# A selective scan: weighings on GpSimd, five polynomial steps on VectorE, front products first on TensorE, two pairs of input banks

## The chip, the core and the metric

The kernel runs on one core of a Trainium2 chip. The metric is the device time of one execution in microseconds. Times of runs are medians; one further execution was taken with the hardware profiler, and all rows below come from that one.

## The reference

Two transformer-like layers over x of shape (8, 512, 128). Layer 0 is a differential attention and a feed-forward network; layer 1 is a selective scan and a mixture of 64 experts. The change lies in the scan (and in one step at the end of the feed-forward network, which prepares the first batch of the scan):

```python
u = silu(conv3(h, conv_w))                     # h: layer-normed x, modulated; 3 taps over time
Bcoeff, Ccoeff = split(u @ W_bc + b_bc)        # 16 + 16 rows over time
A = -exp(A_log)
dt = softplus((u @ W_dt + b_dt) @ W_dtp + b_dtp)
# for each of the N = 16 states n, along time t:
#   h_n[t] = exp(A[:, n] * dt[t]) * h_n[t-1] + Bcoeff[n, t] * dt[t] * u_or_h[t]
y = sum_n Ccoeff[n, t] * h_n[t]  +  h * Dcoeff
x = x + gate * y
```

## The kernel before

The program is a sequence of phases: attention, feed-forward network, scan, experts. Inside a phase each engine has its own list of instructions and the engines meet by semaphores only; the order on an engine is the order in which the code is written. The feature axis (128) lies on the partitions and the 512 time steps along the free axis.

**Rounds and pairs.** The function `scan` runs one round for each of the 8 batches, r = 0 to 7, and a short last one. In a round the 16 states are taken in 8 pairs, m = 0 to 7, so that a tile of a pair is 128x1024. Flags tell what else a round does: `ahead` (r up to 5) prepares batch r + 2, `back` (r up to 6) finishes the step length of batch r + 1, `post` (r from 1) finishes the output of batch r - 1.

**What happens with a pair.** SyncE loads the rows of B and C, spread over all partitions, into `brow` and `crow`, 512 KB each, two places each (L1538); in rounds 0 to 3 its queue also carries the experts' weights, behind pairs 2 and 5. ScalarE makes `dA` = exp(A dt), two places (L1701). VectorE makes `dBx` = dtxb * brow in PSUM, in a single place (`enter`, L1739), and runs the scan over `dA` and `dBx` (`run`, L1749). The states of even pairs go to `gate_a0`, those of odd pairs to two places of `hs`. Even pairs are weighed with C by VectorE: `ch` = gate_a0 * cb (L1756), where `cb` is a copy of `crow` in PSUM, made by ScalarE (L1705). Odd pairs are weighed by GpSimd, straight from `hs` and `crow` (L1592). TensorE adds the `ch` tiles up in PSUM with an identity matrix (`add_pair`, L1630), two pairs behind.

**What else is in a round.** The step length is a softplus: ScalarE makes `zb` and `ee` = exp(-|z|); a polynomial in `ee` of 10 coefficients gives log(1 + ee). GpSimd begins it: one first step (L1198), then six pairs of a product and an addition (L1203, L1204) and a last product (L1208), spread between its four weighings; each instruction waits for the one before it through a semaphore. VectorE does the last two steps after pair 6 (L1186, `pl` = (pl + c) * ee), then `dt` = max(zb, 0) + pl (L1187) and `dtxb` = dt * hT in PSUM (L1189). VectorE normalizes batch r + 2 after pair 0 (`front.norm`, L1019, four instructions on 128x128) and adds the residual after pair 7 (L1729, one input in PSUM). In round 0 it also makes the statistics of batches 4 to 7. TensorE turns, convolves and projects the batch ahead (`turn`, `conv`, `bc_rows`, `z`) in between the sums; `silu` on ScalarE loads an activation table before and after. In rounds 1 to 6 ScalarE and GpSimd also split the experts' weights into two f16 parts (GpSimd: L1585, after weighing 7).

The end of the feed-forward phase does the same polynomial for batch 0 on GpSimd and VectorE, beside the last gating (`w_experts` <- sine, L1432, four instructions; the tiles of the expert weights are lent to that phase, hence the name) and `relu` (L1363).

## Time and profile before

| | us |
|---|---|
| median of 3 runs | 1761.32 (1758.82 to 1764.29) |
| profiled execution | 1767.51 |
| its span, first to last instruction | 1765.5 |
| mean granted clock of TensorE | 0.875 |
| busy in the span: TensorE, VectorE, ScalarE, GpSimd | 1325.0, 1247.3, 1064.9, 891.0 |
| scan phase in it, first to last scan | 995.0 to 1322.6 |

No engine is busy all the time, and each phase has another bound; for the change only the rows of the scan and of the end of the phase before it count. In rows in order of time the first number is the start, the second the time that the row covers; "x2" behind it are two instructions merged in one row. A number in square brackets is how long the engine was idle before, and for whom. Two rows of one engine can overlap by about 0.1 us.

### The profile page before, as it was taken

Reading aid. Unit: us, or ns where it says so; the run is one execution under the profiler, and the core shown is the slowest. Engines: PE = TensorE matmul, PEld = TensorE weight load, DVE = VectorE, ACT = ScalarE, POOL = GpSimd, SP = SyncE. Lnnn points to the kernel's source line nnn. Section 1 sums busy time; section 2 is a strip of 40 time slices with the busy share of each in tenths; the row PEclk is TensorE's granted clock in tenths of the full one; section 3 lists DMA queues with packets and bytes.
Section 4 is the critical chain, followed back from the end, with each engine's and each line's share of the span. In section 5 each row is a group of like instructions: output and inputs, shape, how many; then the busy total and the mean of one; then the engine's idle time right before and its main releaser. Section 6 shows DMA issues by size and latency. Waiting matters only on the chain. (4 is left out here: it accounts for less than half of the span.)

```text
span 1765.5 us, 29658 instructions
## 1 busy us (share of the span) xinstructions
PE 1325.0 (75%) x8526; PEld 587.4 (33%) x8589; DVE 1247.3 (71%) x2064; ACT 1064.9 (60%) x1633; POOL 891.0 (50%) x849
## 2 busy tenths in 40 slices
PE   4587888888888888764665466766555898988898
PEld 3233333333333333332333222222222344444443
DVE  4667767676767667853787688888994666665654
ACT  2277666666667676653554445555533677776686
POOL 3033525252525252433886355565632666766677
PEclk8599999999999899986787777787887999999999
DMA  4231313131313132100000476665654666765675
GB/s 130 72 114 46 106 34 106 37 108 38 108 40 99 42 89 63 39 2 0 1 0 1 133 225 217 221 221 201 210 202 98 164 171 163 184 168 153 173 191 131
DMA packets 123690, 198.73 MB, mean 113 GB/s; under 512 B 24604, under 2 KB 60088, under 8 KB 123576
## 3 DMA queue, kind: packets, MB, share of 16 engines
q1 hardware_dynamic: 122136, 195.08, 38.3%
q10 hardware_dynamic: 1440, 2.10, 0.4%
q8 instruction: 76, 1.25, 0.3%
q14 instruction: 38, 0.31, 0.1%
HBM read 167.76 MB, written 28.84 MB: 111 GB/s over the span
## 5 line engine op out<-in xcount | busy, mean ns | idle before, releaser
L959 DVE TENSOR_REDUCE bmax<-p1b 128x4 f32<-128x512 f32 x640 | 410.8, 685 | 140.1 <-PE p1b L704 135.4
L642 ACT ACTIVATE pT<-p2b 128x512 f32<-128x512 f32 x640 | 349.1, 602 | 193.4 <-PE p2b L756 192.2
L1918 POOL TENSOR_TENSOR hid_l<-e_hid,hid_h 128x1024 f16<-128x1024 f32 (+1 forms) x136 | 281.1, 2075 | 132.0 <-ACT hid_h L2060 131.4
L2176 DVE TENSOR_TENSOR e_hid<-ub,share 128x1024 f32<-128x1024 f32 x128 | 156.1, 1223 | 150.4 <-ACT ub L2073 129.4
L593 POOL CAST nsp<-qneg 128x16 bf16<-128x16 f32 x64 | 12.6, 197 | 442.9 <-DVE qneg L970 442.9
L1630 PE MATMUL yb<-ch,ident 128*128 128x512 f32 x256 | 156.3, 750 | 66.4 <-POOL ch L1592 52.1
L771 PE MATMUL ob<-pT,vs 128*32 128x512 f32 (+3 forms) x2048 | 194.7, 468 | 1.9 <-POOL pT L602 1.2
L2073 ACT ACTIVATE ub<-ub 128x1024 f32<-128x1024 f32 x128 | 129.2, 1009 | 82.5 <-PE ub L1974 80.7
L756 PE MATMUL p2b<-qs,ks 50*128 50x512 bf16 (+3 forms) x1024 | 131.1, 315 | 56.9 <-ACT pT L642 44.8
L2060 ACT ACTIVATE hid_h<-e_hid 128x1024 f16<-128x1024 f32 (+1 forms) x136 | 139.2, 1024 | 25.2 <-DVE e_hid L2176 25.1
L602 POOL TENSOR_SCALAR_AFFINE_SELECT pT<-pT 128x1280 f32<-128x1280 f32 (+2 forms) x192 | 145.0, 787 | 11.5 <-ACT pT L642 11.5
L704 PE MATMUL p1b<-ks,qs 48*128 48x128 bf16 (+2 forms) x1792 | 134.0, 255 | 14.6 <-DVE bmax L959 14.2
L1592 POOL TENSOR_TENSOR ch<-hs,crow 128x1024 f32<-128x1024 f32 x32 | 75.3, 2352 | 137.4 <-DVE hs L1749 96.4
L1972 PE MATMUL ub<-e_hTh,w_high 128*128 (+1 forms) x256 | 100.5, 393 | 22.2 <-DVE e_hid L2176 22.2
L708 PE MATMUL p1b<-causal,identb 128*128 128x512 bf16 x193 | 82.3, 428 | 40.3 <-DVE bmax L959 27.1
L1630 PEld LDWEIGHTS yb<-ch,ident 128*128 128x128 f32 x256 | 56.0, 233 | 157.0 <-issue 67.1
L1972 PE MATMUL e_yb<-hid_h,w_high 128*128 128x512 f16 x264 | 101.6, 385 | 4.7 <-POOL hid_l L1918 3.9
L756 PEld LDWEIGHTS p2b<-qs,ks 50*128 50x128 bf16 x1024 | 34.7, 95 | 209.2 <-ACT pT L642 137.6
L1701 ACT ACTIVATE dA<-dt,nA 128x511 f32<-128x511 f32 (+1 forms) x128 | 84.6, 710 | 28.5 <-DVE gate_a L1749 15.4
L1973 PE MATMUL e_yb<-hid_l,w_high 128*128 128x512 f16 x264 | 101.3, 384 | 0.0
L1974 PE MATMUL e_yb<-hid_h,w_low 128*128 128x512 f16 x264 | 101.0, 382 | 0.0
L1973 PE MATMUL ub<-e_hTl,w_high 128*128 (+1 forms) x256 | 100.5, 393 | 0.0
(263 smaller groups left out, 2530.6 us busy)
## 6 DMA issues: line engine op xcount, KB each, us to landing
share<-shares SPq DMA_DIRECT2D x256, 256.0 KB, 4.1
brow<-bc_rows SPq DMA_DIRECT2D x64, 512.0 KB, 5.3
crow<-bc_rows SPq DMA_DIRECT2D x64, 512.0 KB, 5.2
q_stacks<-parts SPq DMA_DIRECT2D x96, 128.0 KB
k_stacks<-parts SPq DMA_DIRECT2D x96, 128.0 KB
qs<-q_stacks SPq DMA_DIRECT2D x128, 96.0 KB, 2.3
ks<-k_stacks SPq DMA_DIRECT2D x128, 96.0 KB, 2.3
qs<-nparts SPq DMA_DIRECT2D x128, 4.0 KB
```

Of the source, the lines that this page charges most:

```text
L602: pool.affine_select(out=block_ap, in_=block_ap, compare_op=ALU.is_ge, fill=0.0, base=0, pattern=[[0, n], [1, P]], channel_multiplier=-1). ...
L642: act.activation(pT[:, g2 % 2, stored(w), :], p2b[bank_of(g2, w)][:, :], ACT.Exp, scale=SCALE).then_inc(exp_done, 1)
L704: return pe.matmul(bank[:, at * P:(at + blocks[1] - blocks[0]) * P], qs[rows, slot, head, c * P:(c + 1) * P], ks[rows, slot, head, blocks[ ...
L756: mm = pe.matmul(p2b[bank_of(g, 2 * t + j)][:, at:at + S - c * P], ks[rows, slot, head, c * P:(c + 1) * P], qs[rows, slot, head, c * P:S], ...
L771: mm = pe.matmul(ob[32 * m:32 * m + 32, q0:q1], vs[:, a, c, m // 2, :], pT[:, a, u, at:at + q1 - q0], start=(n == 0), stop=(n == len(CHUNK ...
L959: dve.tensor_reduce(to, bank, AX, ALU.max).then_inc(first_read, 1)
L1630: mm = pe.matmul(yb[:, :], k.ident[:, :], ch[:, m % 4, j, :], start=False, stop=(m == PAIRS - 1 and j == 1), skip_group_check=True)
L1918: pool.tensor_tensor(flat(hid_l[:, place(p), 0:n, :]), flat(hid[:, place(p), 0:n, :]), flat(hid_h[:, place(p), 0:n, :]), ALU.subtract).the ...
L1972: pe.matmul(to, w[0], high, start=start, stop=False, skip_group_check=True)
L1973: pe.matmul(to, w[0], low, start=False, stop=False, skip_group_check=True)
L2060: act.activation(flat(hid_h[:, place(p), 0:n, :]), flat(hid[:, place(p), 0:n, :]), ACT.Copy).then_inc(hid_rounded, 1)
L2176: dve.tensor_tensor(h, u, flat(share[:, p % SHARES, :, :]), ALU.mult).then_inc(hid_ready, 1)
```

## The change

- All eight weighings of a round go to GpSimd, straight from the states and `crow`; VectorE's weighing, ScalarE's copy `cb` and its semaphores are gone. The states rotate through three places (`gate_a0`, `hs` 0, `hs` 1), `crow` through four, and `dBx` has two pairs of banks in PSUM. So dBx of pair m + 1 no longer waits for the scan of pair m, and a scan waits for the weighing three pairs before.
- GpSimd begins the polynomial after weighing 0, and does three of the pairs of product and addition instead of six, all before weighing 3. VectorE does five steps instead of two: two after pair 4, two after pair 5, one after pair 6, followed by `dt` and `dtxb` as before.
- GpSimd normalizes batch r + 3 in rounds 0 to 4, two tiles after weighing 3 and two after weighing 4, and batch 2 at the start of round 0. The split of weights stands ahead of weighing 7 instead of behind it.
- TensorE: `turn` at m = 0, `conv` at 2, `bc_rows` at 3 and `z` at 5, each ahead of the sum of its place.
- No round runs in a hardware loop any more (before, rounds 4 and 5 did).

```diff
-LOG_DVE = 2
+LOG_DVE = 5
...
+    def log_steps(self, dve, b, first, last):
+        if first == 0:
+            dve.wait_ge(self.poly_ready, b + 1)
+        link = Chain(dve, self.dve_pre, b * LOG_DVE + first).link
+        for c in LOG1P[LOG_DVE - 1::-1][first:last]:
+            link(dve.scalar_tensor_tensor(self.pl[:, :], self.pl[:, :], c, self.ee[:, :], ALU.add, ALU.mult))
+
     def step_length(self, dve, b):
-        dve.wait_ge(self.poly_ready, b + 1)
-        link = Chain(dve, self.dve_pre, b * LOG_DVE).link
-        for c in LOG1P[LOG_DVE - 1::-1]:
-            link(dve.scalar_tensor_tensor(self.pl[:, :], self.pl[:, :], c, self.ee[:, :], ALU.add, ALU.mult))
...
-        brow, crow = sb("brow", [P, 2, 2, S]), sb("crow", [P, 2, 2, S])
+        brow, crow = sb("brow", [P, 2, 2, S]), sb("crow", [P, C_RING, 2, S])
...
-        cb, dBx = ps("cb", 2), ps("dBx", 2)
-        hs_even = k.gate_a0[:, :, :].rearrange("p b d -> p (b d)")
+        dBx = [ps(f"dBx{i}", 2) for i in range(2)]
+        states = [k.gate_a0[:, :, :].rearrange("p b d -> p (b d)"), flat(hs[:, 0, :, :]), flat(hs[:, 1, :, :])]
...
+                if r == 0:
+                    front.norm(pool, 2)
+                later = r + 3 < B
+                for m in range(PAIRS):
+                    weigh_states(m)
+                    if back and m == 0:
+                        front.log_start(pool, r + 1)
+                        poly_first(pool, front, chain)
+                        poly_more(pool, front, chain, LOG_MORE[0])
+                    if back and m == 1:
+                        poly_more(pool, front, chain, LOG_MORE[1])
+                    if back and m == 2:
+                        poly_more(pool, front, chain, *LOG_MORE[2:])
+                        poly_end(pool, front, chain)
+                    if later and m == 3:
+                        if r == 1:
+                            pool.wait_ge(front.dve_stats, 2 * STATS_LINKS)
+                        front.norm(pool, r + 3, 0, TILES // 2)
+                    if later and m == 4:
+                        front.norm(pool, r + 3, TILES // 2, TILES)
+                    if back and post and m == 6:
+                        split_weights(r - 1)
...
                 for m in range(PAIRS):
+                    if ahead and m == 0:
+                        front.turn(pe, b)
+                    if ahead and m == 2:
+                        pe.wait_ge(x_ready, r)
+                        front.conv(pe, b)
+                    if ahead and m == 3:
+                        front.bc_rows(pe, b)
+                    if ahead and m == 5:
+                        front.z(pe, b)
                     if m == Y_LAG:
                         y_start()
...
-                    if m % 2 == 0 and n % 2:
-                        act.wait_ge(c_loaded[0], (r * HALF + m // 2 + 1) * 16)
-                        act.wait_ge(ch_ready, r * HALF + m // 2 + 1)
-                        act.activation(flat(cb[:, :, :]), flat(crow[:, 0, :, :]), ACT.Copy).then_inc(c_copied, 1)
...
                     if m + 1 < PAIRS:
                         enter(m + 1)
-                    if m % 2 == 0:
-                        weigh_states(m)
                     if not post and m == 0:
                         front.stats(dve, range(4, B))
-                    if ahead and m == 0:
-                        front.norm(dve, r + 2)
                     if post and m == PAIRS - 1:
                         residual()
+                    if back and m >= PAIRS - 4:
+                        at = m - (PAIRS - 4)
+                        front.log_steps(dve, r + 1, min(2 * at, LOG_DVE), min(2 * at + 2, LOG_DVE))
                     if back and m == PAIRS - 2:
                         front.step_length(dve, r + 1)
```

GpSimd in round 1, up to its third weighing. Before (the names are output <- inputs; `ch` is a weighing, `pl` the polynomial):

```order
L1198 TENSOR_SCALAR pl<-ee 128x512
L1203 TENSOR_TENSOR pl<-pl,ee 128x512
L1204 TENSOR_SCALAR pl<-pl 128x512
L1592 TENSOR_TENSOR ch<-hs,crow 128x1024
L1203 TENSOR_TENSOR pl<-pl,ee 128x512
L1204 TENSOR_SCALAR pl<-pl 128x512
L1203 TENSOR_TENSOR pl<-pl,ee 128x512
L1204 TENSOR_SCALAR pl<-pl 128x512
L1592 TENSOR_TENSOR ch<-hs,crow 128x1024
```

And after, from the first weighing of the round to the fourth:

```order
L1604 TENSOR_TENSOR ch<-gate_a,crow 128x1024
L1205 TENSOR_SCALAR pl<-ee 128x512
L1210 TENSOR_TENSOR pl<-pl,ee 128x512
L1211 TENSOR_SCALAR pl<-pl 128x512
L1604 TENSOR_TENSOR ch<-hs,crow 128x1024
L1210 TENSOR_TENSOR pl<-pl,ee 128x512
L1211 TENSOR_SCALAR pl<-pl 128x512
L1604 TENSOR_TENSOR ch<-hs,crow 128x1024
L1210 TENSOR_TENSOR pl<-pl,ee 128x512
L1211 TENSOR_SCALAR pl<-pl 128x512
L1215 TENSOR_TENSOR pl<-pl,ee 128x512
L1604 TENSOR_TENSOR ch<-gate_a,crow 128x1024
```

What moved: a weighing now opens the round, the polynomial ends right ahead of weighing 3, and weighing 3 waits for nothing that the polynomial makes. What follows on GpSimd in the same round, after:

```order
L1022 TENSOR_SCALAR s_xn<-x_tok,stats,rstd 128x128
L1022 TENSOR_SCALAR s_xn<-x_tok,stats,rstd 128x128
L1604 TENSOR_TENSOR ch<-hs,crow 128x1024
L1022 TENSOR_SCALAR s_xn<-x_tok,stats,rstd 128x128
L1022 TENSOR_SCALAR s_xn<-x_tok,stats,rstd 128x128
L1604 TENSOR_TENSOR ch<-hs,crow 128x1024
L1604 TENSOR_TENSOR ch<-gate_a,crow 128x1024
L1597 TENSOR_TENSOR w_low<-w_experts,w_high 128x2x704
```

The normalizing stands around weighing 4, and the split of weights behind weighing 6. VectorE from pair 6 of a round to pair 0 of the next, before (the scan has the name SCALAR_TENSOR_TENSOR here):

```order
L1749 SCALAR_TENSOR_TENSOR gate_a<-dA,dBx 128x1024
L1739 TENSOR_TENSOR dBx<-dtxb,brow 128x1024
L1756 TENSOR_TENSOR ch<-gate_a,cb 128x1024
L1186 SCALAR_TENSOR_TENSOR pl<-pl,ee 128x512 x2
L1187 SCALAR_TENSOR_TENSOR dt<-zb,pl 128x512
L1189 TENSOR_TENSOR dtxb<-dt,s_hT 128x512
L1749 SCALAR_TENSOR_TENSOR hs<-dA,dBx 128x1024
L1729 TENSOR_TENSOR x_tok<-x_tok,s_pre 128x512
```

And after, from pair 4 on:

```order
L1749 TENSOR_TENSOR dBx<-dtxb,brow 128x1024
L1191 SCALAR_TENSOR_TENSOR pl<-pl,ee 128x512 x2
L1758 SCALAR_TENSOR_TENSOR hs<-dA,dBx 128x1024
L1749 TENSOR_TENSOR dBx<-dtxb,brow 128x1024
L1191 SCALAR_TENSOR_TENSOR pl<-pl,ee 128x512 x2
L1758 SCALAR_TENSOR_TENSOR gate_a<-dA,dBx 128x1024
L1749 TENSOR_TENSOR dBx<-dtxb,brow 128x1024
L1191 SCALAR_TENSOR_TENSOR pl<-pl,ee 128x512
L1194 SCALAR_TENSOR_TENSOR dt<-zb,pl 128x512
L1196 TENSOR_TENSOR dtxb<-dt,s_hT 128x512
L1758 SCALAR_TENSOR_TENSOR hs<-dA,dBx 128x1024
```

The weighing is gone, and the polynomial steps stand between scans 4, 5, 6 and 7.

## Rows read from the trace of the kernel before

**Rows 1.** Stretches of the scan: length, then busy us of each engine, clock, DMA.
```profile
995.00:1038.70 43.70, 24.55 (x46) 8.98 (x46) 39.40 (x57) 22.35 (x31) 18.95 (x15) 0.73 0.72 231
1038.70:1211.00 172.30, 116.65 (x216) 44.01 (x216) 149.21 (x117) 96.06 (x129) 98.76 (x76) 0.78 0.67 215
1211.00:1253.30 42.30, 28.50 (x54) 10.74 (x54) 37.50 (x30) 24.39 (x34) 25.34 (x20) 0.78 0.57 200
1253.30:1290.30 37.00, 20.05 (x38) 7.61 (x38) 35.52 (x25) 17.97 (x24) 25.19 (x20) 0.82 0.66 227
1290.30:1325.00 34.70, 21.93 (x38) 8.13 (x38) 31.61 (x20) 11.41 (x16) 12.81 (x6) 0.77 0.58 197
```

**Rows 2.** VectorE in order of time, the last scan of the phase.
```profile
1320.34 2.28 DVE L1749 TENSOR_TENSOR_SCAN hs<-dA,dBx 128x1024 f32<-128x1024 f32 x1
```

**Rows 3.** VectorE in order of time, end of round 1 and start of round 2.
```profile
1075.22 1.41 DVE L1186 SCALAR_TENSOR_TENSOR pl<-pl,ee 128x512 f32<-128x512 f32 x2
...
1077.39 0.70 DVE L1189 TENSOR_TENSOR dtxb<-dt,s_hT 128x512 f32<-128x512 f32 x1
1078.00 2.28 DVE L1749 TENSOR_TENSOR_SCAN hs<-dA,dBx 128x1024 f32<-128x1024 f32 x1
1080.20 0.66 DVE L1729 TENSOR_TENSOR x_tok<-x_tok,s_pre 128x512 f32<-128x512 f32 x1
1080.78 1.22 DVE L1739 TENSOR_TENSOR dBx<-dtxb,brow 128x1024 f32<-128x1024 f32 x1
1082.11 2.29 DVE L1749 TENSOR_TENSOR_SCAN gate_a<-dA,dBx 128x1024 f32<-128x1024 f32 x1
...
1085.67 1.21 DVE L1756 TENSOR_TENSOR ch<-gate_a,cb 128x1024 f32<-128x1024 f32 x1
1086.80 2.08 DVE L1019 TENSOR_SCALAR s_xn<-x_tok,stats,rstd 128x128 f32<-128x128 f32 x4
```

**Rows 4.** GpSimd in order of time, the same stretch.
```profile
1080.42 2.35 POOL L1592 TENSOR_TENSOR ch<-hs,crow 128x1024 f32<-128x1024 f32 x1 [5.37 <-issue]
1082.73 2.86 POOL L1585 TENSOR_TENSOR w_low<-w_experts,w_high 128x1408 f16<-128x1408 f32 x1
1085.67 0.62 POOL L1198 TENSOR_SCALAR pl<-ee 128x512 f32<-128x512 f32 x1
1086.47 1.26 POOL L1203 TENSOR_TENSOR pl<-pl,ee 128x512 f32<-128x512 f32 x1 [0.18 <-POOL pl L1198]
1087.93 0.62 POOL L1204 TENSOR_SCALAR pl<-pl 128x512 f32<-128x512 f32 x1 [0.20 <-POOL pl L1203]
```

**Rows 5.** VectorE's polynomial steps, one line: count, duration ns min/median/max, first and last start.
```profile
L1186 DVE SCALAR_TENSOR_TENSOR pl<-pl,ee x16: 682/691/692, 976.0 to 1284.2; 128x512 f32<-128x512 f32 x16
```

**Rows 6.** VectorE in the experts: one line's instructions, then two in order of time.
```profile
L68 DVE SCALAR_TENSOR_TENSOR e_rstd<-e_rtmp,e_rstd x24: 161/164/1979, 1332.4 to 1653.0; 128x4 f32<-128x4 f32 x24
...
1390.04 1.98 DVE L68 SCALAR_TENSOR_TENSOR e_rstd<-e_rtmp,e_rstd 128x4 f32<-128x4 f32 x1
...
1427.44 1.42 DVE L2143 TENSOR_TENSOR rest<-rest,biased 128x256 f32<-128x256 f32 x1
```

**Rows 7.** GpSimd in order of time at the same two places.
```profile
1389.88 2.12 POOL L1918 TENSOR_TENSOR hid_l<-e_hid,hid_h 128x1024 f16<-128x1024 f32 x1 [0.90 <-ACT hid_h L2060]
...
1424.36 6.49 POOL L1918 TENSOR_TENSOR hid_l<-e_hid,hid_h 128x1024 f16<-128x1024 f32 x3 [2.67 <-ACT hid_h L2060]
```

**Rows 8.** GpSimd by form: busy us, mean ns of one, an instruction on 128x128.
```profile
L301 POOL TENSOR_SCALAR_AFFINE_SELECT ident<-ident 128x128 f32<-128x128 f32 x1 | 0.3, 292 | 0.2 <-POOL ones L298 0.2
```

**Rows 9.** End of the feed-forward phase: VectorE's gating, GpSimd's first step, the gating's line.
```profile
966.62 5.46 DVE L1432 SCALAR_TENSOR_TENSOR w_experts<-sine,coef,w_experts 128x512 f32<-128x512 f32 x4 [5.24 <-ACT sine L1346]
...
958.98 0.62 POOL L1198 TENSOR_SCALAR pl<-ee 128x512 f32<-128x512 f32 x1 [13.29 <-ACT ee L1149]
...
L1432 DVE SCALAR_TENSOR_TENSOR w_experts<-sine,coef,w_experts x32: 737/1092/1762, 843.5 to 971.0; 128x512 f32<-128x512 f32 x16, 128x512 f32 x16
```

**Rows 10.** The 64 loads of brow: us from issue to landing.
```profile
DMA to landing us min/median/max: 3.7/5.3/9.3
```

More of the change, by code:

```diff
@@ L1161, in log_start, with norm @@
         pool.sem_inc(self.pool_passed, 1)
-    def norm(self, dve, b):
+    def norm(self, dve, b, first=0, last=TILES):
         if self.later(b):
             dve.wait_ge(self.xT_done, b)
-        for c in range(TILES):
+        for c in range(first, last):
             ins = normalize(dve, self.k, self.xn[:, c, :], b * TILES + c)
-        ins.then_inc(self.xn_ready, 1)
+        if last == TILES:
+            ins.then_inc(self.xn_ready, 1)
     def stats(self, dve, batches):
@@ L1455, in step @@
                 if ends(r, 1):
+                    front.log_steps(dve, 0, 0, LOG_DVE)
                     front.step_length(dve, 0)
@@ L1477, in scan @@
     PAIRS = N // 2
-    HALF = PAIRS // 2
+    C_RING = 4
+    C_USES = PAIRS // C_RING
+    HS_RING = 3
     with ExitStack() as ctx:
@@ L1598, in step @@
[L1598 to L1610 removed]
+                    q = r * PAIRS + m
@@ L1653, in step @@
                         add_pair(r - 1, m - Y_LAG + PAIRS)
-                    if ahead and m == 1:
-                        front.turn(pe, b)
-                    if ahead and m == 2:
-                        pe.wait_ge(x_ready, r)
-                        front.conv(pe, b)
-                    if ahead and m == 4:
-                        front.bc_rows(pe, b)
-                    if ahead and m == 5:
-                        front.z(pe, b)
                     if post and m == PAIRS - 2:
```

76 lines of the change are left out of this document (24 added, 52 removed).

## The prediction

> **What bounds the kernel now.** I read, in this order: the stretches of the scan, then VectorE's and GpSimd's instructions in order of time through one round, then the places elsewhere in the trace where these two engines run side by side. The scan runs from 995.0 to 1322.6 us. In the table of stretches [rows 1] the reader is to see that VectorE is busy 149.2 of 172.3 us in rounds 1 to 4, ScalarE 96.1 and GpSimd 98.8: VectorE bounds the stage and idles 5.8 us a round. The rounds last 43.7 (round 0), 4 x 43.1, 42.3 and 37.0 us from first scan to first scan; round 7 takes 1290.3 to the end of its last scan, 1320.3 + 2.3 = 1322.6, so 32.3 [rows 1, 2]. The order in time [rows 3] gives the distances from start to start that I use on VectorE: scan to the next instruction that does not need it 2.20; dBx to the scan that needs it 1.33; dBx otherwise 1.25; two polynomial steps and dt 2.17 (1075.22 to 1077.39), so 0.72 each; dtxb 0.61; the residual 0.58. GpSimd's [rows 4]: weighing to the next instruction 2.31 (its record is 2.35 long), first step 0.80, product to addition 1.46, addition to next 0.80, so a pair 2.26; the split of weights 2.86.
>
> **What is taken away and added, if nothing collided.** In a round VectorE loses four weighings (1085.67 to 1086.80 in steps of 1.13: 4.5 us) and the normalizing (2.08 us) [rows 3], and with a second bank for dBx the wait between a scan and the next dBx. It gains three polynomial steps, 2.2 us. ScalarE loses four copies of crow; at 96.1 busy of 172.3 us it is not the bound [rows 1], and I count nothing. A scan with its dBx is then 2.20 + 1.33 = 3.53 us. Eight of them, five steps, dt, dtxb and the residual are 28.2 + 3.6 + 1.3 + 0.6 = 33.8 us a round. TensorE's front products come ahead of the sums; the states have three places, ch four, and by my times their next writer comes over 2 us after their last reader, so I count nothing there.
>
> **Where it collides.** The step is pl<-pl,ee: two inputs in SBUF, none in PSUM. In this trace 16 of them took 0.682 to 0.692 us [rows 5], because GpSimd idled then, waiting for the next scan. Where GpSimd does run, a VectorE instruction with two SBUF inputs waits for it: e_rstd on 128x4, median 0.164 us, took 1.98, from 1390.04 to 1392.02, while GpSimd's hid_l ran from 1389.88 to 1392.00; and rest on 128x256, asked for at 1427.44, ended at 1428.86, so it got in between two of three hid_l that stood back to back, which together took 6.49 instead of 3 x 2.13 = 6.39 [rows 6, 7]. So the later one waits, VectorE gets in 0.14 us before the end of GpSimd's record, GpSimd's next one starts 0.1 before the end of VectorE's, and they take turns. Scans and dBx have one input in PSUM and keep 2.28 and 1.22 beside the split and a weighing [rows 3, 4]. The Trainium skill has this as a rule (SBUF — State Buffer, Who interferes with whom): the pair of ports that the two engines share is a lock for a whole instruction, and one operand in PSUM avoids it. The trace agrees (1.98 against 0.16 us); it speaks against moving steps to VectorE, and the sum by it is the one I work out.
>
> **A round with turns (rounds 1 to 4), from the end of scan 0.** GpSimd: 0.1, three weighings 6.9, first step 0.8, three pairs 6.8, last product 1.3: the polynomial is ready at 15.9 [rows 4]. VectorE comes at 15.4 and starts step 1 just after GpSimd has begun weighing 3 (15.9 to 18.25), so step 1 gets in at 18.1 and ends at 18.8. One normalizing instruction of 0.35 us goes between, step 2 ends at 19.65. Scan 5 and dBx 6 end at 23.1; by then weighing 4 (19.9 to 22.25) and two normalizings (0.7) are over and weighing 5 runs from 22.95 to 25.3: step 3 ends at 25.85, step 4 beside an idle GpSimd at 26.55. Scan 6 ends at 28.8, weighing 6 runs to 31.2, step 5 ends at 31.75. GpSimd's split then runs to 34.5 and dt behind it ends at 35.05. dtxb 0.65, scan 7 2.2, residual 0.6, dBx 1.35, scan 0 2.2: 42.1 us. The unclear price is the normalizing on GpSimd, 128x128 with two scalars per partition. Nearest rows: 0.29 for another 128x128 instruction [rows 8] and 0.62 for an addition on 128x512 [rows 4]; I take 0.35, near the first. Four of them lie on the path: at 0.2 a round is 0.6 shorter, at 0.62 1.1 longer. That step 1 slips in ahead of weighing 3 is the other end there: then step 2 waits instead, which changes a round with normalizing by about nothing and rounds 5 and 6 by -2.
>
> **The other rounds.** Rounds 5 and 6 have no normalizing left on GpSimd, so step 2 waits for the whole of weighing 4: 43.1 us each. Round 0 has the statistics of four batches on VectorE, which collide with the polynomial and push scan 1 to 7.1, weighing 3 to 22.15 and, with no split and no residual, the round to 42.7. Round 7 has no steps: 7 x 3.53 + 2.28 = 27.0.
> The sum: round 0 42.7 - 43.7 = -1.0; rounds 1 to 4 168.4 - 172.3 = -3.9; round 5 43.1 - 42.3 = +0.8; round 6 43.1 - 37.0 = +6.1; round 7 27.0 - 32.3 = -5.3. The stage: -3.3 us.
> **Ahead of the scan** the shorter polynomial helps: the last four w_experts instructions, 5.46 us from 966.62, take turns with it; one alone takes 0.74 [rows 9]. The polynomial now ends at 958.98 + 0.80 + 3 x 2.26 + 1.27 = 967.8; one wait of 1.1, then 0.69 + 3 x 0.74, ends them at 970.6, not 972.1. relu on ScalarE needs them, and the last products of the phase need relu: -1.5 us. VectorE's three steps more there, 2.2 us, come after those instructions and only lead to dt; I count them as free, and were they on the path the total would be 2.2 higher.
> Total -4.8 against the profiled execution's 1767.5 us, of which 1765.5 is span and 2.0 lies around it. That execution is 6.2 over the median of the runs; I apply the difference to the median 1761.3: **1756.5 us**.
>
> **Cover that I count on.** VectorE waits from 15.4 to 18.1 in each round, 2.7 us. In it must fit what comes late in scans 1 to 4: ScalarE's silu with two table loads, and brow, whose time from issue to landing is 3.7 to 9.3, median 5.3 [rows 10]: it is issued at the end of dBx m-2, 5.8 us ahead of dBx m, and in rounds 0 to 3 704 KB of weights go in front of brow 3. I take that delay as 1 to 2 us, hidden; round 7 has no weights, but no cover either.
>
> **Rivals.** (1) VectorE is not held: the 33.8 us above, with step 1 at 16.0, make rounds 34.4. Round 0 -4.9, rounds 1 to 4 -34.7, rounds 5 and 6 -10.5, round 7 -5.3: about -55, 1706 us. For it: the 16 steps of [rows 5] were never slow. Against it: rows 6, 7 and 9, where just such instructions wait. 0.08. (2) The normalizing is dear on GpSimd, since no row shows an instruction with pointers there. Each 0.1 costs 0.4 a round in five rounds, 2.0; it decides from 0.35 + 4.8/20 = 0.59, and at twice the 0.62 of an addition, 1.24, gives +13: 1774. 0.10. (3) VectorE does not get its turn behind a weighing because GpSimd's next is queued: steps 1 and 2 come at 22, +3 in seven rounds, +16: 1777. Against it the 6.49 of [rows 7]. 0.05. (4) The front of rounds 0 to 3 comes late by 5 to 6 us, past the cover of 2.7 (brow behind the weights, or silu behind TensorE at 1.2 GHz): +3 x 4 = 12, 1768. For it: a landing of 9.3 us is in the rows [rows 10]. Against it: that is the longest of 64, the median is 5.3. 0.09. That the change doesn't do what it says I exclude: the order of the instructions shows each move.
>
> **How the numbers follow.** The forecast has 0.68; its own range is -9 to +2, 1752 to 1763. What a measurement tells from no change is about 0.3%, 5.3 us, so below 1756.0 is faster. The forecast lies 0.5 above: of its 0.68, 0.32 faster, 0.33 same, 0.03 slower. Rival 1 adds 0.08 to faster, rivals 2 to 4 0.01 to faster, 0.02 to same, 0.21 to slower: 0.41, 0.35, 0.24. The range 1748 to 1772 holds the forecast, rival 4 and the lower half of rival 2; outside it are rivals 1 and 3 and the rest of 2, some 0.18.
>
> **What would show it.** Right: pl<-pl,ee (0.69 before) with a mean near 1.8 us and a maximum near 2.9, dt near 3.3 in rounds 1 to 6; rounds 1 to 4 near 42, round 6 longer than before by 6, round 7 near 27; scans 2.28 and dBx 1.23 unchanged, 3.53 apart. Wrong: steps of 0.69 beside weighings (rival 1); s_xn on GpSimd over 0.6 (2); step 1 later than 19 us after scan 0 (3); VectorE waiting for brow or dA in rounds 0 to 3 for over 3 us (4); w_experts' last four still 5.4 us.

## The result and the profile after

| | before | after |
|---|---|---|
| median of 11 runs each | 1763.8 us (1756.2 to 1770.9) | 1753.9 us (1744.8 to 1758.9) |
| ratio | | 0.9940, 95% interval 0.9917 to 0.9964 |
| profiled execution, its span | 1767.5, 1765.5 us | 1750.9, 1749.1 us |
| scan phase in it, first scan to the end of the last | 995.0 to 1322.6: 327.6 | 989.0 to 1306.0: 317.1 |

The change takes off 0.6%, 10.6 us by the ratio (6.3 to 14.6). The forecast was 4.8, under half of it, although the forecast time, 1756.5 us, is only 2.6 us above the measured median. The stretches of the scan in the changed kernel, which answer to [rows 1] (length, then busy us and number of instructions of TensorE, its weight loads, VectorE, ScalarE, GpSimd; granted clock, DMA share, GB/s): round 0, rounds 1 to 4, rounds 5, 6 and 7.

```profile
988.99:1030.24 41.25, 25.07 (x45) 9.20 (x46) 39.52 (x53) 17.01 (x25) 28.75 (x20) 0.79 0.76 257
1030.24:1192.16 161.92, 108.49 (x218) 40.86 (x217) 153.59 (x96) 81.53 (x113) 133.77 (x85) 0.86 0.68 229
1192.16:1235.72 43.56, 28.40 (x52) 10.10 (x50) 41.73 (x24) 20.29 (x28) 29.89 (x18) 0.77 0.56 194
1235.72:1279.25 43.53, 24.20 (x38) 8.72 (x38) 41.73 (x25) 13.89 (x19) 29.85 (x18) 0.74 0.58 193
1279.25:1306.04 26.79, 17.81 (x37) 6.62 (x38) 26.16 (x16) 8.69 (x13) 17.15 (x8) 0.92 0.70 235
```

GpSimd went from 98.8 to 133.8 us in rounds 1 to 4. VectorE went from 149.2 to 153.6 although it lost four weighings and the normalizing a round and gained only three steps: a recorded duration includes the time for which an instruction is held (a step has 0.68 us at the least in the first row below, 2.82 at the most). The rounds, with each term of the forecast's sum:

| | before | forecast | after | against before |
|---|---|---|---|---|
| round 0 | 43.7 | 42.7 | 41.25 | -2.4 |
| rounds 1 to 4, each | 43.1 | 42.1 | 40.48 | -10.4 in all |
| round 5 | 42.3 | 43.1 | 43.56 | +1.2 |
| round 6 | 37.0 | 43.1 | 43.53 | +6.5 |
| round 7 | 32.3 | 27.0 | 26.79 | -5.5 |
| stage | 327.6 | 324.3 | 317.1 | -10.6 (forecast -3.3) |

VectorE's polynomial steps and dt, by line (count, ns min/median/max, first and last start), which answer to [rows 5]:

```profile
L1191 DVE SCALAR_TENSOR_TENSOR pl<-pl,ee x40: 677/824/2815, 973.0 to 1269.3; 128x512 f32<-128x512 f32 x40
...
L1194 DVE SCALAR_TENSOR_TENSOR dt<-zb,pl x8: 691/3217/3220, 976.6 to 1271.3; 128x512 f32<-128x512 f32 x8
```

Round 3 in order of time, from the end of the polynomial on, VectorE (start, length, instruction; "x2" are two in one row):

```profile
1128.80 1.21 DVE L1749 TENSOR_TENSOR dBx<-dtxb,brow 128x1024 f32<-128x1024 f32 x1
1129.91 3.54 DVE L1191 SCALAR_TENSOR_TENSOR pl<-pl,ee 128x512 f32<-128x512 f32 x2
1133.49 2.29 DVE L1758 TENSOR_TENSOR_SCAN hs<-dA,dBx 128x1024 f32<-128x1024 f32 x1
...
1136.81 1.54 DVE L1191 SCALAR_TENSOR_TENSOR pl<-pl,ee 128x512 f32<-128x512 f32 x2
...
1141.70 2.00 DVE L1191 SCALAR_TENSOR_TENSOR pl<-pl,ee 128x512 f32<-128x512 f32 x1
1143.73 3.22 DVE L1194 SCALAR_TENSOR_TENSOR dt<-zb,pl 128x512 f32<-128x512 f32 x1
```

And GpSimd:

```profile
1128.47 1.27 POOL L1215 TENSOR_TENSOR pl<-pl,ee 128x512 f32<-128x512 f32 x1 [0.18 <-PE yb L1644]
1129.71 2.34 POOL L1604 TENSOR_TENSOR ch<-gate_a,crow 128x1024 f32<-128x1024 f32 x1
1132.04 2.08 POOL L1022 TENSOR_SCALAR s_xn<-x_tok,stats,rstd 128x128 f32<-128x128 f32 x2
1134.09 2.34 POOL L1604 TENSOR_TENSOR ch<-hs,crow 128x1024 f32<-128x1024 f32 x1
1136.42 1.73 POOL L1022 TENSOR_SCALAR s_xn<-x_tok,stats,rstd 128x128 f32<-128x128 f32 x2
1138.12 2.44 POOL L1604 TENSOR_TENSOR ch<-hs,crow 128x1024 f32<-128x1024 f32 x1
1140.80 2.35 POOL L1604 TENSOR_TENSOR ch<-gate_a,crow 128x1024 f32<-128x1024 f32 x1 [0.24 <-issue]
1143.11 3.29 POOL L1597 TENSOR_TENSOR w_low<-w_experts,w_high 128x1408 f16<-128x1408 f32 x1
```

The reader is to see three holds. Step 1 waits for weighing 3 (3.54 us for two steps that take 1.41 alone). Step 5 waits for weighing 6 (2.00 for one). dt waits for the split (3.22 instead of 0.69). Steps 3 and 4 are the exception: 1.54 us for two while GpSimd normalizes. The forecast had step 3 wait for weighing 5 there.

At the end of the feed-forward phase the four last gating instructions answer to [rows 9], 5.46 us before:

```profile
963.94 3.74 DVE L1439 SCALAR_TENSOR_TENSOR w_experts<-sine,coef,w_experts 128x512 f32<-128x512 f32 x4 [5.24 <-ACT sine L1353]
```

### The profile page after: what moved, and what is told of

The parts are those of the page before. It is cut to its first block and busy times, and to the rows that moved or that the text cites. A ratio compares the mean times of both kernels' runs of the same rounds, so it can differ in the third digit from the quotient of the medians.

```text
span 1749.1 us, 29225 instructions
## 1 busy us (share of the span) xinstructions
PE 1316.7 (75%) x8526; PEld 583.7 (33%) x8589; DVE 1256.6 (72%) x2032; ACT 1035.4 (59%) x1601; POOL 945.3 (54%) x857
## 5 line engine op out<-in xcount | busy, mean ns | idle before, releaser
L1715 ACT ACTIVATE dA<-dt,nA 128x511 f32<-128x511 f32 x128 | 85.0, 712 | 114.5 <-DVE hs L1758 73.1
L704 PE MATMUL p1b<-ks,qs 48*128 48x128 bf16 (+2 forms) x1792 | 133.7, 255 | 14.6 <-DVE bmax L959 14.1
L1604 POOL TENSOR_TENSOR ch<-hs,crow 128x1024 f32<-128x1024 f32 x40 | 95.3, 2383 | 45.4 <-DVE hs L1758 40.7
```

## Experiments

All but the first and the seventh (the kernel before, once more) are changes to the changed kernel. The versions have 4 to 12 runs each. Ratios are against runs of the kernel before on the same chip (its median 1763.8 us beside the changed kernel, 1764.7 to 1765.6 beside the others). Since the phases around the scan differ from execution to execution by several us (see the last section), the last columns tell the length of the scan phase and of its rounds 1 to 4, 5 and 6 in the profiled execution.

| | median us | ratio (95%) | scan phase | rounds 1 to 4 | 5, 6 |
|---|---|---|---|---|---|
| changed kernel | 1753.9 | 0.9940 (0.9917 to 0.9964) | 317.1 | 40.48 | 43.5 |
| e1 split after dt | 1731.4 | 0.9817 (0.9794 to 0.9840) | 302.1 | 37.98 | 41.1 |
| e2 normalizing on VectorE | 1767.1 | 1.0018 (1.0000 to 1.0036) | 334.8 | 43.67 | 43.6 |
| e3 give way | 1723.5 | 0.9759 (0.9727 to 0.9792) | 291.7 | 36.7 to 37.8 | 37.5 |
| e4 first batch as before | 1757.2 | 0.9961 (0.9941 to 0.9981) | 317.4 | 40.5 to 40.8 | 43.5 |
| e5 two steps | 1790.6 | 1.0153 (1.0118 to 1.0188) | 350.7 | 47.0 | 44.2 |
| e6 six steps | 1716.5 | 0.9720 (0.9685 to 0.9754) | 283.2 | 35.4 to 37.1 | 36.0, 35.2 |
| e7 before, once more | 1768.5 (one run) | | 326.5 | 42.0 to 44.0 | 42.7, 37.2 |
| e8 one bank | 1752.0 | 0.9919 (0.9892 to 0.9946) | 320.0 | 40.71 | 43.6 |
| e9 sums first | 1750.4 | 0.9920 (0.9891 to 0.9949) | 317.1 | 40.49 | 43.6 |

### The two engines by themselves

A program of its own with two lists of instructions, one per engine, that start together in each case:

```python
cases = [([norm] * 4 + [const] * 4 + [weigh] * 2, []),      # (1) GpSimd's list, VectorE's list
         ([], [step] * 4 + [pstep] * 4 + [vnorm] * 4),      # (2)
         ([weigh] * 6, [step] * 6),                         # (3)
         ([const] * 12, [step] * 10),                       # (4)
         ([norm] * 12, [step] * 10),                        # (5)
         ([weigh] * 6, [pstep] * 10),                       # (6) first input in PSUM
         ([weigh] * 6, [vnorm] * 10)]                       # (7) one input, with constants
```

> Only a measurement of what VectorE and GpSimd do to each other; none of the reference is computed and the output is zeros. Seven cases, between which the two engines meet. (1) GpSimd alone: four normalizings 128x128 with two scalars per partition, four products-and-additions with constants 128x512, two weighings 128x1024. (2) VectorE alone: four polynomial steps with both inputs in SBUF, four with one input in PSUM, four instructions with one SBUF input. (3) Six weighings beside six steps. (4) Twelve GpSimd instructions with one input and constants beside steps. (5) Twelve normalizings beside steps. (6) Weighings beside steps with one input in PSUM. (7) Weighings beside VectorE instructions with one input. My theory: a GpSimd instruction with two SBUF inputs and a VectorE instruction with two SBUF inputs exclude each other for their whole length and alternate, so case 3 lasts 6 x 2.35 + 6 x 0.69 = 18.2 us and a step there is recorded near 2.9; a GpSimd instruction with one tensor input holds nobody up, so in cases 4 and 5 the steps keep 0.69 and the two lists overlap (the normalizings stood beside two steps for 1.54 us in the changed kernel); cases 6 and 7 overlap, too. Rival A: every GpSimd instruction holds the ports: in case 5 each step is recorded near 0.8 + 0.7 = 1.5 us, in case 4 near 1.3. Rival B: nothing is excluded and steps are slow in the scan for another reason: 0.69 in all cases.

Measured, in order of time; L37 is the step, L38 the step with one input in PSUM, L39 VectorE's instruction with one input, L34 the weighing, L36 GpSimd's with constants, L35 the normalizing:

```profile
6.95 3.13 POOL L35 TENSOR_SCALAR xn<-x_tok,stats 128x128 f32<-128x128 f32 x4 [3.73 <-DVE zero L73]
10.05 2.38 POOL L36 TENSOR_SCALAR pgo<-pg 128x512 f32<-128x512 f32 x4
12.39 4.64 POOL L34 TENSOR_TENSOR ch<-hs,crow 128x1024 f32<-128x1024 f32 x2
17.07 2.50 DVE L37 SCALAR_TENSOR_TENSOR plo<-pl,ee 128x512 f32<-128x512 f32 x4 [10.22 <-POOL ch L34]
...
21.87 1.42 DVE L39 TENSOR_SCALAR dvn<-pl 128x512 f32<-128x512 f32 x4
23.33 14.42 DVE L37 SCALAR_TENSOR_TENSOR plo<-pl,ee 128x512 f32<-128x512 f32 x6
23.38 16.57 POOL L34 TENSOR_TENSOR ch<-hs,crow 128x1024 f32<-128x1024 f32 x6 [6.35 <-DVE dvn L39]
39.98 9.83 DVE L37 SCALAR_TENSOR_TENSOR plo<-pl,ee 128x512 f32<-128x512 f32 x10 [2.23 <-POOL ch L34]
40.03 11.42 POOL L36 TENSOR_SCALAR pgo<-pg 128x512 f32<-128x512 f32 x12
51.49 6.39 DVE L37 SCALAR_TENSOR_TENSOR plo<-pl,ee 128x512 f32<-128x512 f32 x10 [1.68 <-POOL pgo L36]
51.56 13.21 POOL L35 TENSOR_SCALAR xn<-x_tok,stats 128x128 f32<-128x128 f32 x12
64.80 6.07 DVE L38 SCALAR_TENSOR_TENSOR plo<-pb,ee 128x512 f32<-128x512 f32 x10 [6.92 <-POOL xn L35]
...
78.73 16.30 DVE L39 TENSOR_SCALAR dvn<-pl 128x512 f32<-128x512 f32 x10 [7.86 <-POOL ch L34]
```

- Weighings and steps take turns: 2.76 us for one of each (16.57/6), near 2.32 + 0.62 = 2.94 from the cases alone. The median step there is recorded with 2.82 us; in case 2, alone, four took 2.50.
- One input in PSUM: 0.61 us a step beside weighings, 0.62 alone. Not held.
- The normalizing does not hold steps: 0.64 us a step beside it against 0.62 alone. It is the normalizing that waits: the twelve took 13.21 us, where four alone took 3.13, and the longest was recorded with 2.33 us instead of 0.79.
- Two points of the theory fell. GpSimd's one-input instruction with constants does take turns with steps (0.98 us a step). So it is not the number of inputs that sets the normalizing apart, but something in its own form or its small size, which these cases do not separate. And VectorE's instruction with one input in SBUF waits as well: ten took 16.30 us beside six weighings, where four alone took 1.42.

Rival B (nothing excluded) is out; rival A (every GpSimd instruction holds) holds for all but the normalizing.

### The split behind dt

```diff
                 def split_weights(c):
                     pool.wait_ge(k.w_rounded, c + 1)
+                    pool.wait_ge(front.dtx_ready, r + 2)
```

> The changed kernel with one more wait: GpSimd's split of the weights waits until dtxb of the round is made. Theory (turns): dt stands 3.22 us only because the split, 2.86, runs beside it. GpSimd idled 3.6 us behind the split, so it can run later at no cost: dt falls to 0.7, dtxb stays 0.7, and rounds 1 to 6 are 2.5 us shorter each: 38.0 in rounds 1 to 4, 41.0 in 5 and 6; the stage is 15 us shorter, 1739 us where the changed kernel has 1754. Rival A (dt is slow for another reason, ScalarE's zb or the semaphores between): dt stays at 3.2 and the time at 1754. Rival B (the split then makes weighing 7 and with it the sums late, or brow cannot follow): dt falls to 0.7 but rounds stay over 39.5, gain under 6 us.

VectorE and then GpSimd in round 3 of this kernel, in order of time:

```profile
1136.71 2.00 DVE L1191 SCALAR_TENSOR_TENSOR pl<-pl,ee 128x512 f32<-128x512 f32 x1
1138.74 0.69 DVE L1194 SCALAR_TENSOR_TENSOR dt<-zb,pl 128x512 f32<-128x512 f32 x1
1139.46 0.70 DVE L1196 TENSOR_TENSOR dtxb<-dt,s_hT 128x512 f32<-128x512 f32 x1
...
1140.31 2.87 POOL L1598 TENSOR_TENSOR w_low<-w_experts,w_high 128x1408 f16<-128x1408 f32 x1 [2.15 <-DVE dtxb L1196]
```

dt took 0.69 instead of 3.22 us, the rounds 37.98 and 41.1 where 38.0 and 41.0 were expected, and the stage 14.9 us less, where 15 were. Both rivals are out. One wait that makes GpSimd idle for 2.15 us takes more off the scan than the whole change did (14.9 against 10.6 us). The median, 1731.4, is below the 1739 expected: the medians differ by 22 us, more than the stage explains; 6.0 us of it are, in the profiled execution, the experts' phase (437.1 against 443.1 us), whose code is the same. Whether that is chance was not settled.

### The normalizing back on VectorE

```diff
 GpSimd:
-                if r == 0:
-                    front.norm(pool, 2)
...
-                        front.norm(pool, r + 3, 0, TILES // 2)
...
-                        front.norm(pool, r + 3, TILES // 2, TILES)
 VectorE:
+                if r == 0:
+                    front.norm(dve, 2)
                 enter(0)
...
+                    if r + 3 < B and m == 1:
+                        front.norm(dve, r + 3)
```

> The changed kernel with the normalizing back on VectorE: batch 2 ahead of round 0, batch r + 3 after pair 1 of rounds 0 to 4; GpSimd loses 16 to 20 instructions of 0.79 to 0.87 us, 3.3 us a round. Theory: on GpSimd they hold nobody up and keep weighings 4 and 5 out of the way of steps 2 to 4. Without them step 2 waits for weighing 4 and steps 3 and 4 for weighing 5, as in rounds 5 and 6 of the changed kernel, while their 2.1 us on VectorE lie half in its wait for the polynomial (1.2 us): rounds 1 to 4 go from 40.5 to 43.5 or a little more, 12 us in all, 1766 us. Rival (the forecast's own way of counting): four normalizings lie on the path with about 0.8 each and come off it, and 2.1 us on VectorE come in the cover of the wait: rounds 1 to 4 fall to 38 to 39.5, 1744 to 1750 us.

VectorE in round 3 of this kernel:

```profile
1129.76 3.63 DVE L1022 TENSOR_SCALAR s_xn<-x_tok,stats,rstd 128x128 f32<-128x128 f32 x4
...
1143.62 3.57 DVE L1191 SCALAR_TENSOR_TENSOR pl<-pl,ee 128x512 f32<-128x512 f32 x2
...
1150.54 2.73 DVE L1191 SCALAR_TENSOR_TENSOR pl<-pl,ee 128x512 f32<-128x512 f32 x2
```

The rounds are 43.67, 3.2 us longer, as the theory has it, and round 0 is 5.0 longer, which it did not have. The working behind the number was half right. Steps 3 and 4 cost 2.73 instead of 1.54, because weighing 5 now starts right behind scan 5: 1.2 us. Steps 1 and 2 did not get dearer (3.57 against 3.54); the other 2.0 us are that VectorE arrives at step 1 later, 20.7 us after the start of scan 0 instead of 18.7. Its normalizing took 3.63 us instead of 2.08, held by GpSimd like the one-input instruction of case 7, and the cover of the wait for the polynomial was not long enough. The rival, by which GpSimd's normalizing lies on the path at its full price, is out.

### GpSimd gives way

```diff
+    GIVE_WAY = {4: 2, 5: 4}
...
                 def weigh_states(m):
                     q = r * PAIRS + m
+                    if back and m in GIVE_WAY:
+                        pool.wait_ge(front.dve_pre, (r + 1) * LOG_DVE + GIVE_WAY[m])
+                    if back and m == PAIRS - 2:
+                        pool.wait_ge(front.dtx_ready, r + 2)
```

(and the split's wait for `dtx_ready`, as in e1.)

> The split waits for dtxb as in the run before, and three weighings give way too: weighing 4 waits for step 2, weighing 5 for step 4, weighing 6 for dtxb. Theory: of the steps only the first still waits for a weighing (1.4 to 2.1 us); GpSimd has the slack (it idled 3.6 + 1.7 us at the round's end). By an arithmetic of the two engines with turns rounds 1 to 6 are 36.5 to 38.5, the stage 25 to 32 us shorter than in the changed kernel: 1722 to 1730. Rival A (GpSimd becomes the bound: its weighings 6 and 7 and the split end so late that weighing 0 and the polynomial of the next round are): rounds of 39 to 41, no better than the split's wait alone, 1738 to 1745. Rival B: brow, issued two pairs ahead, cannot follow a round of under 39 us: VectorE waits for brow for 2 us or more a round, 1735 to 1740.

Rounds 5 and 6 fell from 43.5 to 37.5 us, the stage by 25.4. In round 3 step 5 and dt are no longer held:

```profile
1135.79 0.68 DVE L1191 SCALAR_TENSOR_TENSOR pl<-pl,ee 128x512 f32<-128x512 f32 x1
1136.50 0.69 DVE L1194 SCALAR_TENSOR_TENSOR dt<-zb,pl 128x512 f32<-128x512 f32 x1
```

What is left is step 1 behind weighing 3. VectorE also waited 8.3 us for the polynomial in all. Rivals A and B show as small waits only, in the whole scan: 2.3 us for brow, leaving out the one ahead of the first scan, 1.7 for a weighing, 1.6 for dA.

### The first batch's polynomial as before

```diff
-        for c in LOG1P[LOG_DVE - 1::-1][first:last]:
+        for c in LOG1P[(LOG_DVE if b else FIRST_DVE) - 1::-1][first:last]:
...
-                    poly_more(pool, front, chain, *LOG_MORE)
+                    poly_more(pool, front, chain, *FIRST_MORE)
```

with `FIRST_DVE` = 2.

> The changed kernel, but the polynomial of batch 0, at the end of the feed-forward phase, is divided as before: six pairs of product and addition on GpSimd, two steps on VectorE. In the traces the last four gating instructions lasted 5.46 us before and 3.74 after; from their start to the last f_gated it was 19.43 us before and 16.35 after, 3.1 us apart, where the forecast had 1.5. Theory: the gating is 1.7 us longer, relu and with it silu come later, TensorE idles 2.9 us instead of 1.1 ahead of its products for B, C and dt and runs them at the lower clock level: 1.92 and 1.54 us for two pairs instead of 1.04 and 1.02, another 1.4. So gating 5.46, those products 1.92 and 1.54, and the first scan at 992 where the changed kernel has 989.0; total +3 us, 1757. Rival A (the forecast's term): only +1.5, products still 1.04 and 1.02. Rival B (the phase was shorter because of something earlier in the program that differs from run to run): the first scan stays at 989, total 1754.

The gating and TensorE's products for B, C and dt in this kernel, then the products in the changed kernel:

```profile
967.98 5.46 DVE L1446 SCALAR_TENSOR_TENSOR w_experts<-sine,coef,w_experts 128x512 f32<-128x512 f32 x4 [5.24 <-ACT sine L1360]
...
977.45 1.92 PE L1126 MATMUL s_preb<-us,wbc 128*32 128x512 f32 x2 [2.88 <-ACT us L1141]
979.16 1.51 PE L1127 MATMUL s_pre<-us,wdt 128*8 128x512 f32 x2
```

```profile
971.70 1.04 PE L1119 MATMUL s_preb<-us,wbc 128*32 128x512 f32 x2 [1.13 <-ACT us L1134]
972.58 1.02 PE L1120 MATMUL s_pre<-us,wdt 128*8 128x512 f32 x2
```

From the start of the gating to the start of the last f_gated it is 19.38 us here, 16.35 in the changed kernel, and 19.43 before: 3.0 us, of which the gating is 1.7. The other 1.3 is how much longer these products took, with TensorE at the lower clock. It had idled 2.88 us instead of 1.13 ahead of them. The two stretches below, the products' in the kernel before and then in the changed one, tell length, busy us and matmuls of TensorE, and then the granted clock: 0.61, so mostly 1.2 GHz, against 1.00, 2.4 GHz. In this version it was 0.59.

```profile
976.10:979.60 3.50, 3.25 (x4) 0.61 0.01 2
```

```profile
971.70:973.90 2.20, 1.90 (x4) 1.00 0.00 0
```

The median rose by 3.3 us, as expected, though that alone is less than the measurement can tell. Rival A is out. The first scan stood at 996.0, not at 992: this execution was 4.0 us late already when the gating started, in code that is the same. So rival B is wrong for the 3 us, and right in that such shifts exist.

### Two steps on VectorE

```diff
-LOG_DVE = 5
+LOG_DVE = 2
...
-                    if back and m == 1:
-                        poly_more(pool, front, chain, LOG_MORE[1])
-                    if back and m == 2:
-                        poly_more(pool, front, chain, *LOG_MORE[2:])
+                    if back and 1 <= m <= 5:
+                        poly_more(pool, front, chain, LOG_MORE[m])
+                    if back and m == 5:
                         poly_end(pool, front, chain)
...
-                    if back and m >= PAIRS - 4:
-                        at = m - (PAIRS - 4)
-                        front.log_steps(dve, r + 1, min(2 * at, LOG_DVE), min(2 * at + 2, LOG_DVE))
                     if back and m == PAIRS - 2:
+                        front.log_steps(dve, r + 1, 0, LOG_DVE)
                         front.step_length(dve, r + 1)
```

> The changed kernel with two polynomial steps on VectorE as before, both after pair 6, and the six pairs of product and addition on GpSimd one behind each of weighings 0 to 5; the rest of the change stays. Theory: GpSimd then has 40.3 us of work in rounds 1 to 4 (eight weighings 18.5, polynomial 15.6, normalizing 3.2, split 2.9), the polynomial is ready behind weighing 5 only, 33 us after scan 0 and 5 after VectorE wants it; an arithmetic of the two engines with turns gives rounds of 47 (rounds 1 to 4) and 44 (5 and 6), 22 us more in all: 1776 us, slower than before the change. That would say that the three steps, though each waits for a weighing, are worth more than they cost. Rival: the steps' waits of 6 us a round are the cost of the change and without them rounds are no longer than 40.5: 1754 or less.

VectorE's waits in this kernel (who waited for whom: us in all, times, longest):

```profile
DVE pl L1191 <- POOL pl L1215: 66.1, 7, 11.2
```

Rounds of 47.0 and 44.2 us as worked out, and the rival is out: the medians are 37 us apart, and without the three steps on VectorE, VectorE waits 66.1 us for GpSimd's polynomial. The expected 22 us more and 1776 us were too low: those rounds against the measured 40.5 and 43.5 already make 27, and round 0 is 6.1 longer, 47.3 instead of 41.25. The stage is 33.7 longer.

### Six steps, in turns

```diff
-LOG_DVE = 5
+LOG_DVE = 6
...
+    GIVE_WAY = {3: 2, 5: 4}
...
                     if back and m == 2:
-                        poly_more(pool, front, chain, *LOG_MORE[2:])
                         poly_end(pool, front, chain)
-                    if later and m == 3:
+                    if later and m == 5:
...
-                        front.norm(pool, r + 3, 0, TILES // 2)
-                    if later and m == 4:
-                        front.norm(pool, r + 3, TILES // 2, TILES)
+                        front.norm(pool, r + 3)
```

with the waits of `weigh_states` and of the split from the version above.

> A version that uses the turns: six steps on VectorE, two each after pairs 4, 5 and 6, two pairs of product and addition on GpSimd; weighing 3 waits for step 2, weighing 5 for step 4, weighing 6 for dtxb, the split stands behind it; the normalizing of GpSimd stands behind weighing 5. Theory: no VectorE instruction waits for GpSimd longer than 0.7 us; the arithmetic with turns gives 35.2 us for rounds 1 to 6 against 37.7 with the version that gives way and has five steps; the stage 272 to 280 us, 1706 to 1712 in all. Rival A: DMA is the bound from there (8 MB of brow and crow and 0.7 MB of weights a round; its share was 0.73 in the version with 37.7 us): VectorE waits for brow 1 to 3 us a round, 1715 to 1722. Rival B: ScalarE's and TensorE's front cannot make a batch ahead in 35 us: waits for dA or ee of over 1 us a round, also 1715 to 1722.

The steps by line, and VectorE's waits in the scan and right ahead of it:

```profile
L1191 DVE SCALAR_TENSOR_TENSOR pl<-pl,ee x48: 674/692/1929, 973.9 to 1239.2; 128x512 f32<-128x512 f32 x48
```

```profile
DVE dBx L1752 <- DMA brow<-bc_rows: 7.2, 3, 5.3
DVE hs L1761 <- ACT dA L1718: 2.2, 4, 0.9
DVE hs L1761 <- POOL ch L1610: 1.7, 6, 0.3
```

The median of a step is 0.692 us again (0.824 in the changed kernel), but the theory's 0.7 us as the longest wait was too low: steps 3 and 4 took 2.65 us for two in five of the seven rounds, beside weighing 4, which does not give way. The kernel takes 1716.5 us: 2.8% faster than before, 37 us below the changed kernel. The expectation was missed, though. The stage is 283.2 us, 3 above the range expected, and the median lies not in 1706 to 1712 but where both rivals had it, 1715 to 1722.

Of the 7.2 us for brow, 5.3 is the one ahead of the first scan that every version has. The other 1.9, and 2.2 for dA, come in rounds 2, 3 and 5: 4.1 us, as much as the miss of the stage, and short of the 1 us in every round that the rivals asked for. So both rivals are there in a small way, and neither is the bound. DMA's share is 0.76 from 990 to 1267 us.

### The kernel before, once more

> The kernel before, once more, only for a second trace of it: the first one was a slow execution (1767.5 against a median of 1763.8), and its last four gating instructions started 2.7 us later than those of the changed kernel, in code that both have. Theory (execution to execution): here they start at 964 to 967, gating lasts 5.46 again and the first scan comes 28.4 us behind their start, as in the first trace. The scan's rounds are 43.7, 43.4, 43.5, 41.7, 43.7, 42.3, 37.0 and 32.3 within 0.5. Rival: the 2.7 us belong to the change (its tiles lie elsewhere in memory): again 966.6.

The gating started at 971.36 and took 5.47 us, the first scan came at 999.85, 28.5 behind. The expected start of 964 to 967 was missed, and the rival's 966.6 too: the start in equal code varies by more than I thought. Rounds 0, 2 and 4 are 1.0 shorter, 0.5 longer and 1.6 shorter than in the first trace, so two of the eight missed their 0.5; the stage is 326.5 against 327.6. So the kernel before varies in its scan by about 1 us, and the changed kernel stands 9.5 to 10.6 below it there.

### One pair of banks

```diff
-                    dve.wait_ge(scan_done, r * PAIRS + m + 1)
+                    dve.wait_ge(scan_done, r * PAIRS + m + 2)
...
-        dBx = [ps(f"dBx{i}", 2) for i in range(2)]
+        dBx = [ps("dBx", 2)] * 2
```

> The changed kernel with dBx in one pair of banks again, so that dBx of pair m + 1 waits for scan m. In the first trace of before dBx starts 2.42 us after a scan (1114.01 to 1116.43), in the changed kernel 2.20. Theory: 0.22 us more for each of the seven dBx inside a round; the four ahead of the polynomial lie in VectorE's wait for it (1.2 us a round), the other three do not: 0.7 us in rounds 0 to 6, 1.5 in round 7, where there is no wait: +6 us, 1760. Rival A (nothing hides it): 1.5 us in every round, +12, 1766. Rival B (all is hidden, since the steps behind wait for a weighing anyway): +1.5 in round 7 alone, 1755.

dBx starts 2.42 us after a scan again. The stage is 2.9 us longer: 1.7 in round 7, 0.2 to 0.3 in rounds 0 to 4, nothing in rounds 5 and 6. That is nearest to rival B; my 0.7 for the three dBx behind the polynomial was too much. That what follows them waits for a weighing in any case would explain it; no run shows it by itself. In the median, 1752.0, nothing of it is to be seen.

### Sums first on TensorE

```diff
                 for m in range(PAIRS):
-                    if ahead and m == 0:
-                        front.turn(pe, b)
...
-                    if ahead and m == 3:
-                        front.bc_rows(pe, b)
-                    if ahead and m == 5:
-                        front.z(pe, b)
                     if m == Y_LAG:
                         y_start()
...
+                    if ahead and m == 1:
+                        front.turn(pe, b)
...
+                    if ahead and m == 4:
+                        front.bc_rows(pe, b)
+                    if ahead and m == 5:
+                        front.z(pe, b)
```

(`conv` stays at pair 2, behind the sum as well.)

> The changed kernel with TensorE's order as before: each sum ahead of the front's product of its place, turn at pair 1, B, C and dt at pair 4. Theory (as the forecast counted it): the front has slack, ScalarE's ee waits up to 9.8 us for dt of the batch before in a round, so nothing on VectorE moves: rounds 40.5 and 43.5 again, 1754 within 3 us. Rival (the order was needed): with the sums, which now wait for GpSimd's weighings, in front, silu and the rows of B and C come 3 to 5 us later, and VectorE waits for brow or dA: 1 us a round or more, 1762 or slower.

All rounds are the changed kernel's within 0.02 us. TensorE's new order brings nothing and costs nothing here; the rival is out.

## Why the prediction was right, and which terms were not

**Right.** The mechanism: VectorE's instructions with two SBUF inputs wait for GpSimd's and take turns with them [rows 6, 7]; the cases by themselves show it (2.82 us recorded for a step beside weighings, 0.68 with one input in PSUM) and e1 shows what it costs. The Trainium skill's rule (SBUF — State Buffer, Who interferes with whom) agrees here, but for the normalizing, which no row before showed. As the prediction put it: scans 2.29 and dBx 1.21 to 1.23 unchanged and 3.50 apart (3.53); dt 3.22 (3.3); longest step 2.82 (2.9); step 1 and 2 over at 20.05 us from the end of scan 0 (19.65, since the polynomial came at 16.3, not 15.9); rounds 5 and 6 43.5 (43.1) and round 7 26.8 (27.0). The mean step is 1.44 us, not 1.8 (the row by groups below): five of the 40 stand before the scan, 0.72 each, which leaves 1.54, and ten stand beside normalizings.

```profile
L1191 DVE SCALAR_TENSOR_TENSOR pl<-pl,ee 128x512 f32<-128x512 f32 x40 | 57.6, 1441 | 5.3 <-POOL pl L1215 4.7
```

**Rounds 1 to 4: 42.1 forecast, 40.48 measured.** The step that failed is "by then weighing 4 and two normalizings (0.7) are over and weighing 5 runs from 22.95 to 25.3: step 3 ends at 25.85". From the end of scan 0 of round 3 (1113.40) weighing 5 ran from 24.7 to 27.2 instead, and steps 3 and 4 were over at 24.95, not 26.55. Two errors about one instruction made this. The normalizing takes 0.79 to 0.87 us, not 0.35, past the 0.59 from which rival 2 was to decide; and none of it is on the path, since it does not hold VectorE (0.64 against 0.62 us a step in case 5). By the first error alone a round would be about 1.9 us longer (four times 0.47), 44.0 us, longer than before the change; by both it is 1.6 shorter than forecast, because the longer normalizing keeps weighing 5 away until the steps are through. So it is in part luck that this term came as near as it did: two errors pulled opposite ways. e2 takes the normalizing away and 1.2 us come back at steps 3 and 4. The forecast's bounds for this price, 0.2 to 0.62, came from an affine select and an addition with constants [rows 4, 8]; case 4 shows such an addition to be of another kind, which does take turns with the steps.

**Round 0: -2.4 instead of -1.0.** The same step failed there, in about the same size: steps 3 and 4 took 1.54 us, and the split, which would hold dt, is not there in either account.

**Ahead of the scan: -1.5 forecast, -3.1 in the trace, -3.0 by e4.** The gating term was right in size (3.74, forecast 1.1 + 0.69 + 3 x 0.74 = 4.0). What was missing is that the work behind it gets cheaper when it comes sooner: TensorE idles 1.13 instead of 2.88 us and runs the next four matmuls at 2.4 instead of mostly 1.2 GHz, 1.90 instead of 3.25 us. The three steps added there were free, as counted.

**Together.** -10.6 and -3.1 are -13.7 by the two traces, against a forecast of -4.8 and a measured ratio of -10.6 (-6.3 to -14.6). The profiled executions differ by 16.6; of the other 2.9, 2.7 is a shift ahead of the gating, in code that is the same, and e7 shows that such a shift is no property of the kernel. The interval leaves out the forecast's -4.8, and -10.6 lies outside its own range of -9 to +2. That the forecast time came within 2.6 us owes something to luck: it was set off from a median of 1761.3, and the kernel before had 1763.8 over all eleven runs.

**A wait that the forecast did not name.** It put ScalarE's four copies of `crow` at nothing, since ScalarE is not busy for long. But in the kernel before VectorE waited 17.2 us for dA within rounds 1 to 5 (20.9 in all in e7's trace), once for 3.65:

```profile
1060.71 2.29 DVE L1749 TENSOR_TENSOR_SCAN gate_a<-dA,dBx 128x1024 f32<-128x1024 f32 x1 [3.65 <-ACT dA L1701]
```

In that round ScalarE had stood 5.96 us in front of the copy, for `crow` to land, and 4.22 in front of silu, for TensorE's convolution, both ahead of this dA. The changed kernel has no wait for dA in the scan. The sum for a round after was built up from its instructions and so holds none either; it came out right here without saying why. TensorE's order is not the reason (e9: 1.5 us for dA in all), nor the second pair of banks (e8: none). No run puts the copies or the two places of `crow` back, so whether they made the wait stays open, and with it how much of the gain is theirs.

**Rivals.** 1 (not held) is out: its rounds were 34.4. 2 (dear normalizing) had its premise met and its consequence not. 3 (turn lost behind queued weighings) is out: in case 3 each step got in between two weighings. 4 (brow late) showed 2.08 and 1.28 us in rounds 2 and 3, inside the cover of 2.7, with both rounds at 40.48. Round 6 got 6.5 longer where 6.1 was forecast: it had less to lose before (no normalizing, and no wait for dA), and now its steps and its dt are held like those of round 5 (43.53 and 43.56).

## What to carry to other kernels

Moving work to a second engine loses part of its worth where the two hold each other up; where they do, decide who goes first, with a wait that makes the engine with slack stand back. Here one such wait, that let GpSimd idle for 2 us, took more off the scan than the whole change had, and four of them, with one more step on VectorE and the normalizing in another place, moved 37 us. A recorded duration far above the same form's shortest is the sign to look for; then look at what runs on the other engine at that moment.

An engine that is idle for much of a stage can still be what another waits for: look at the waits, not only at the busy share.

Before a price is bounded by near rows, ask whether those rows are of the same form: here the price was outside its bounds, and what it did to the path had the other sign.
